# A four-layer graph network on one core: index, attribute and node loads of two passes moved from SyncE's queue to ScalarE's, or asked for by rounds

## The reference, cut to what matters

```python
# layer 2: tensor product with 9 attributes of each edge, summed at the target
summand = _tensor_product(x[i], edge_attr, [w0, w1, w2, w3, w4])
out = jax.ops.segment_sum(summand, j, num_segments=x.shape[0])
return out / float(np.sqrt(NUM_NEIGHBORS))

# layer 3: attention with 64 attributes of each edge
e = (edge_features @ W_edge.T).reshape(num_edges, H, HD)
att = jnp.sum(jnp.concatenate([h[src], h[tgt], e], axis=-1) * a, axis=-1)
...
h_prime = jax.ops.segment_sum(w[:, :, None] * h_src, tgt, num_segments=num_nodes)
```

## Time and profile before

| | |
|---|---|
| three runs, median (lowest to highest) | 7131.51 us (7114.65 to 7133.34) |
| profiled execution | 7100.64 us, span 7098.8 us |
| busy share of the span: PE, DVE, ACT, POOL | 65%, 41%, 35%, 53% |
| mean granted TensorE clock | 0.759 of full speed |
| tensor pass, from its first gather to about its end | 1168 to 3378 us |
| attention pass, the same | 3465 to 6177 us |
| issued DMAs of `e_l` | 196 of 256.0 KB |

### The profile page before, as it was taken

How to read it: one execution, slowest core, us unless ns; L and a number is a source line. 1 busy time by engine, 2 the same in 40 slices (tenths; PEclk the granted TensorE clock), 3 DMA queues, 4 the chain that set the end, 5 groups by cost and what they waited for, 6 DMA issues and landing times. The chain is left out here.

```text
span 7098.8 us, 101641 instructions
## 1 busy us (share of the span) xinstructions
PE 4647.0 (65%) x27975; PEld 3696.9 (52%) x27975; DVE 2932.3 (41%) x9168; ACT 2497.3 (35%) x5991; POOL 3759.5 (53%) x3840
## 2 busy tenths in 40 slices
PE   3389883677777777877465565566555655548886
PEld 2255552465565565656454554455445554525555
DVE  6876553343333333332433333333333333441124
ACT  2434442122222222222455454554555445420003
POOL 0367754555555555555355555555555555446664
PEclk7599996788888888888657666665666666668998
DMA  3133432111111111111222222222222222234442
GB/s 58 58 121 125 144 136 72 45 46 41 40 43 43 40 42 44 43 41 42 54 58 58 63 59 57 58 58 61 59 58 58 58 60 59 47 119 142 149 142 78
DMA packets 412220, 493.79 MB, mean 70 GB/s; under 512 B 253185, under 2 KB 311942, under 8 KB 400897
## 3 DMA queue, kind: packets, MB, share of 16 engines
q0 software_dynamic: 120320, 249.88, 14.1%
q1 hardware_dynamic: 289193, 239.52, 11.4%
q10 hardware_dynamic: 2400, 0.57, 0.1%
HBM read 398.36 MB, written 91.05 MB: 69 GB/s over the span
## 5 line engine op out<-in xcount | busy, mean ns | idle before, releaser
L3597 POOL DMA_INDIRECT rows_l<-table,idx_l x1568 | 1484.0, 946 | 1261.5 <-issue 1022.8
L3101 POOL DMA_INDIRECT rows_l<-table,idx_l x1280 | 1212.5, 947 | 1020.8 <-issue 838.5
L3885 PE MATMUL banks_l<-wrow_l,hot_l 128*128 128x136 f32 x3136 | 778.0, 425 | 1086.7 <-DVE wrow_l L3778 751.8
L3885 PEld LDWEIGHTS banks_l<-wrow_l,hot_l 128*128 128x128 f32 x3136 | 708.5, 321 | 1186.1 <-issue 881.5
L1724 POOL DMA_INDIRECT rows_l<-table,row_idx x896 | 945.3, 1055 | 505.0 <-issue 250.3
L3137 ACT COPY agg_l<-ps_l 128x288 f32<-128x288 f32 x640 | 252.8, 404 | 1553.0 <-PE ps_l L3328 628.7
L3368 PE MATMUL pd_l<-d_row_l,d_hot_l 128*128 128x441 f32 x992 | 527.0, 656 | 304.0 <-ACT d_sums_l L3121 215.7
L3343 PE MATMUL pm_l<-w_mix,agg_l 128*128 128x128 f32 x2880 | 487.9, 301 | 120.1 <-ACT msg_l L3149 73.8
L3328 PEld LDWEIGHTS ps_l<-hoty_l,rows_l 128*128 128x128 f32 x2560 | 444.1, 221 | 164.8 <-issue 163.7
L3635 DVE TENSOR_REDUCE score_l<-bank_s_l 128x32 f32<-128x128 f32 x196 | 57.5, 293 | 1142.0 <-DMA rows_l<-table,idx_l 1133.2
L3328 PE MATMUL ps_l<-hoty_l,rows_l 128*128 128x144 f32 x2560 | 492.8, 320 | 32.4 <-issue 21.9
(11 more groups left out here) (628 smaller groups left out, 8451.9 us busy)
## 6 DMA issues: line engine op xcount, KB each, us to landing
e_l<-in_edge_attr SPq DMA_DIRECT2D x196, 256.0 KB
rows_l<-table,idx_l POOLq DMA_INDIRECT x2848
counts_table<-x_nodes SPq DMA_DIRECT2D x22, 1568.0 KB
x_nodes<-counts_table SPq DMA_DIRECT2D x22, 1568.0 KB
counts_table<-h_nodes SPq DMA_DIRECT2D x21, 1568.0 KB
h_nodes<-counts_table SPq DMA_DIRECT2D x21, 1568.0 KB
rows_l<-table,row_idx POOLq DMA_INDIRECT x896
table<-h_nodes SPq DMA_DIRECT2D x21, 448.0 KB
```

The lines of the kernel that those rows point to most:

```text
L3101: pool.indirect_dma_start(out=rows[:, u, j, :], out_offset=None, in_=table, in_offset=bass.IndirectOffsetOnAxis(ap=idx[:, u, j:j + 1], axi ...
L3597: pool.indirect_dma_start(out=rows[:, u, j, :], out_offset=None, in_=table, in_offset=bass.IndirectOffsetOnAxis(ap=idx[:, u, j:j + 1], axi ...
L3885: last = nc.tensor.matmul(p_sum[:, 0:WROW], hot[:, s, j, :], wrow[:, s, j, :], start=(j == 0), stop=(j == J - 1))
```

## The change

In the tensor pass, `idx` now has room for two rounds instead of four groups. SyncE asks for a round's indices with one DMA (128 x 32 values) instead of four (128 x 8), two rounds ahead, when the four `summed` of the older round are up; GpSimd waits for them once a round. `load_dense` moves from SyncE's queue to ScalarE's, where it stands ahead of `take_parts` in a group's step, and the plan puts at most three nodes at a group instead of six, so 78 groups hold loads where 39 did: groups 0 to 11, and then six groups in a row for each batch (30 to 35, 44 to 49, and so on to 139 to 144). In the attention pass the index and edge attribute loads go to ScalarE: the first four of each at the window's start (`load_first`), and the others at the end of ScalarE's step, behind `widen_hots`, for the group four further on (`load_on`). SyncE keeps `ht` and the gates.

```diff
-                while len(self.loads_at[after]) == 6:
+                while len(self.loads_at[after]) == 3:
...
-        idx = sb("idx", [P, U, J], I32)
+        idx = sb("idx", [P, 2, U * J], I32)
...
-                def load_idx(rnd, u):
-                    at = skip * (U * J) + (rnd * U + u) * J
-                    sp.dma_start(idx[:, u, :], core.near_src[:, ds(sp.snap(at), J)]).then_inc(idx_loaded[u], DMA)
+                def load_idx(rnd):
+                    at = skip * (U * J) + rnd * (U * J)
+                    sp.dma_start(idx[:, rnd % 2, :], core.near_src[:, ds(sp.snap(at), U * J)]).then_inc(idx_loaded[rnd % 2], DMA)
...
-                for u in range(U):
-                    load_idx(0, u)
+                load_idx(0)
                 load_raw(0)
+                load_idx(1)
                 sp.dma_start(rel[:, :, :].rearrange("p g j -> p (g j)"),
                              core.near_rel[:, ds(sp.snap(skip * (U * J)), G * J)]).then_inc(rel_loaded, DMA)
                 sp.dma_start(place0[:, :], core.near_place[:, ds(sp.snap(skip * U), G)]).then_inc(place_loaded, DMA)
-                for rnd in range(R):
+                for rnd in range(R - 1):
                     t = w * R + rnd
-                    for u in range(U):
-                        for i in dense.loads_at[rnd * U + u]:
-                            load_dense(w, i)
-                        if rnd == R - 1:
-                            continue
-                        if u == 0:
-                            sp.wait_ge(raw_turned, START + t + 1)
-                            load_raw(rnd + 1)
-                        for q in range(PAIRS):
-                            sp.wait_ge(rows_loaded[u][q], (t + 1) * (2 * DMA))
-                        load_idx(rnd + 1, u)
-            for u in range(U):
-                sp.wait_ge(idx_loaded[u], START + windows * (R * DMA))
+                    sp.wait_ge(raw_turned, START + t + 1)
+                    load_raw(rnd + 1)
+                    if rnd < R - 2:
+                        for u in range(U):
+                            sp.wait_ge(summed[u], START + t + 1)
+                        load_idx(rnd + 2)
...
-                    for u in range(U):
-                        pool.wait_ge(idx_loaded[u], START + t * DMA + DMA)
-                        pool.wait_ge(summed[u], START + t)
-                        pool.sem_inc(group_begun, 1)
-                        for j in range(J):
-                            pool.indirect_dma_start(
-                                out=rows[:, u, j, :], out_offset=None, in_=table,
-                                in_offset=bass.IndirectOffsetOnAxis(ap=idx[:, u, j:j + 1], axis=0),
-                            ).then_inc(rows_loaded[u][j // 2], DMA)
+                with pool.Fori(0, R // 2) as two:
+                    for s in range(2):
+                        t = w * R + two * 2 + s
+                        for u in range(U):
+                            if u == 0:
+                                pool.wait_ge(idx_loaded[s], START + w * (R // 2 * DMA) + two * DMA + DMA)
...
+                            for j in range(J):
+                                at = u * J + j
+                                pool.indirect_dma_start(
+                                    out=rows[:, u, j, :], out_offset=None, in_=table,
+                                    in_offset=bass.IndirectOffsetOnAxis(ap=idx[:, s, at:at + 1], axis=0),
...
+            def load_dense(w, i):
+                k = dense.caps[i]
+                first = dense.place_of(dense.first[i])
+                cols = slice(first, first + k)
+                if i % B == 0 and dense.batch_of(i) >= 2:
+                    act.wait_ge(dense_hot, START + w * (V // RUN) + dense.columns(dense.batch_of(i) - 2).stop // RUN)
+                    act.sem_inc(batch_begun, 1)
+                at = ds(act.value_load(dense.starts[0:1, i:i + 1], min_val=0, max_val=sh.e - dense.most * P), k * P)
+                loaded = dense_loaded[dense.batch_of(i)]
+                act.dma_start(d_src[:, cols], src[at].rearrange("(p j) -> p j", j=k)).then_inc(loaded, DMA)
+                act.dma_start(d_attr[:, cols, :].rearrange("p j c -> p (j c)"),
+                             attr[at, :].rearrange("(p j) c -> p (j c)", j=k)).then_inc(loaded, DMA)
...
             with act.Fori(0, windows) as w:
+                act.wait_ge(dense_hot, START + w * (V // RUN))
+                act.sem_inc(window_loads, 1)
                 take_y(w * R, 0)
                 for g in groups_of(w):
+                    for i in dense.loads_at[g.index]:
+                        load_dense(w, i)
                     take_parts(g, w)
...
-                    at = ds(sp.snap(sh.first_edge(rnd, u)), GROUP)
-                    sp.wait_ge(e_turned[u], START + t)
-                    sp.dma_start(e64[:, u, :], e_attr[at, :].rearrange("(p j) k -> p (j k)", j=J)).then_inc(e_loaded[u], DMA)
...
-            load_loop(sp, win, sh, src, idx, idx_loaded, rows_loaded, load_others)
+            windows = win.count(sp)
+            with sp.Fori(0, windows) as w_:
+                with sp.Fori(0, sh.rounds) as rnd:
+                    load_others(w_, w_ * sh.rounds + rnd, rnd)
...
+            def load_index(rnd, u):
+                at = ds(act.snap(sh.first_edge(rnd, u)), GROUP)
+                act.dma_start(idx[:, u, :], src[at].rearrange("(p j) -> p j", j=J)).then_inc(idx_loaded[u], DMA)
+
+            def load_edges(rnd, u):
+                at = ds(act.snap(sh.first_edge(rnd, u)), GROUP)
+                act.dma_start(e64[:, u, :], e_attr[at, :].rearrange("(p j) k -> p (j k)", j=J)).then_inc(e_loaded[u], DMA)
+
+            def load_first(w_):
+                for u in range(U):
+                    act.wait_ge(weighed[u], START + w_ * sh.rounds)
+                    load_index(0, u)
+                for u in range(U):
+                    act.wait_ge(e_turned[u], START + w_ * sh.rounds)
+                    load_edges(0, u)
+
+            def load_on(g):
+
+                if g is None or g.near(U) is None:
+                    return
+                load_index(g.near(U).rnd, g.u)
+                load_edges(g.near(U).rnd, g.u)
...
             with act.Fori(0, windows) as w_:
+                load_first(w_)
...
                     widen_hots(g)
+                    load_on(g)
```

More of the change, by code:

```diff
@@ L2970, in tensor_pass @@
         place_loaded = sem("place_loaded")
-        idx_loaded = sems("idx_loaded", U)
+        idx_loaded = sems("idx_loaded", 2)
         raw_loaded = sem("raw_loaded")
@@ L2994, in tensor_pass @@
         batch_begun = sem("batch_begun")
+        window_loads = sem("window_loads")
         started = sem("started")
@@ L3025, in _ @@
             sems_of.open(sp)
[L3027 to L3038, removed]
             windows = count_windows(sp)
@@ L3069, in _ @@
                 sp.dma_start(place0[:, :], core.near_place[:, ds(sp.snap(skip * U), G)]).then_inc(place_loaded, DMA)
-                for rnd in range(R):
+                for rnd in range(R - 1):
                     t = w * R + rnd
-                    for u in range(U):
-                        for i in dense.loads_at[rnd * U + u]:
-                            load_dense(w, i)
-                        if rnd == R - 1:
-                            continue
-                        if u == 0:
-                            sp.wait_ge(raw_turned, START + t + 1)
-                            load_raw(rnd + 1)
-                        for q in range(PAIRS):
-                            sp.wait_ge(rows_loaded[u][q], (t + 1) * (2 * DMA))
-                        load_idx(rnd + 1, u)
-            for u in range(U):
-                sp.wait_ge(idx_loaded[u], START + windows * (R * DMA))
+                    sp.wait_ge(raw_turned, START + t + 1)
[5 more added lines that the diff above has]
+            for s in range(2):
+                sp.wait_ge(idx_loaded[s], START + windows * (R // 2 * DMA))
             for b in range(dense.batches):
@@ L3093, in _ @@
             with pool.Fori(0, windows) as w:
-                with pool.Fori(0, R) as rnd:
-                    t = w * R + rnd
-                    for u in range(U):
-                        pool.wait_ge(idx_loaded[u], START + t * DMA + DMA)
-                        pool.wait_ge(summed[u], START + t)
-                        pool.sem_inc(group_begun, 1)
-                        for j in range(J):
-                            pool.indirect_dma_start(
-                                out=rows[:, u, j, :], out_offset=None, in_=table,
-                                in_offset=bass.IndirectOffsetOnAxis(ap=idx[:, u, j:j + 1], axis=0),
-                            ).then_inc(rows_loaded[u][j // 2], DMA)
+                with pool.Fori(0, R // 2) as two:
+                    for s in range(2):
+                        t = w * R + two * 2 + s
+                        for u in range(U):
+                            if u == 0:
```

(6 more changed lines are left out.)

## The result

The changed kernel took 7159.24 us (median of 7 runs, 7147.87 to 7177.57), the kernel before 7131.51 us (7 runs, 7114.65 to 7149.83): a ratio of 1.0045, 95% interval 1.0027 to 1.0063. It is slower by 28 us, where I had forecast 40 (7170, range 7090 to 7280).

A forecast was written before the change was run, and what follows sets the result against it. Bound: the loop of eight gathers, their landing, then L3635 and L3778, with ScalarE partly late in the tensor pass. Terms −20 + 50 + 15 − 5 = +40 us on the median 7131.51 give 7171, forecast 7170, range 7090 to 7280.

The forecast's parts named there:

- Tensor pass, indices by rounds: Tensor pass start: asking early for two rounds of indices shortens index and raw_l waits; −20 us, bounds 0 and −40.
- Tensor pass, node loads on ScalarE: Tensor pass: three node loads ahead of a group's first copy make ScalarE late; +50 us, bounds 0 and 160.
- 2.7 us stick out: Tensor pass: three node loads take 5.1 us, ScalarE idles 2.4 us before the copy, so 2.7 us remain uncovered.
- half of it counts: Tensor pass: half the groups run at the gather loop's pace with room, so 80 of 160 us count.
- Attention pass, indices on ScalarE: Attention pass: ScalarE asks for indices after L3971, sometimes too late for the gather; +15 us, bounds 0 and 94.
- Attention pass, start: Attention pass start: e_l loads asked for first shorten GpSimd's pause before the fifth group; −5 us, 0 to −8.
- ScalarE hides it all: Rival, tensor and attention passes: ScalarE's idle time covers the loads, only the start's gain remains; 7100 us, chance 0.23.
- As slowly as SyncE: Rival, both passes: ScalarE issues loads as slowly as SyncE between gathers, 3 us a node; +270, 7402 us, chance 0.12.
- The pause shrinks: Rival, both passes: a quiet SyncE shortens the pause after eight gathers by 1 us a group; −356, 6780 us, chance 0.08.

The follow-up runs named there:

- the first pair: The changed kernel against the kernel before, as first measured and profiled, in the slower behaviour: 7159.24 against 7131.51 us, ratio 1.0045.
- the extra reads: Only the tensor pass edited, each node's start read three times instead of once, against the kernel before: 5720.50 us, ratio 1.0469.

## Why the prediction came out as it did

**The total.** 28 us measured against 40 forecast looks closer than the working was. One of the four terms came out, one was right in kind and too large, one was nothing, and one had the wrong sign.

**What bounds the kernel.** The reading held for the behaviour it was made from, and the changed kernel's trace shows the same loop. I wrote that TensorE's release reaches VectorE only once the gathers have landed. That is true of those rows, and it was not a property of the kernel: the same program ran without it and 1668 us shorter. What on the chip differed isn't known.

**Tensor pass, indices by rounds: −20.** Measured −17 in the first thirty groups of one profile each, and the index waits are gone. The mechanism is right; how much of the 17 it made isn't separated from the shorter wait for raw_l and from chance. It hangs on SyncE's slowness at the start, and is 0 where SyncE isn't slow.

**Tensor pass, node loads on ScalarE: +50.** Measured +32 in groups 30 to 159, off by 18. The pitch was 1.54 us where I had 1.7. The mechanism, late copies behind a block of loads, is shown by experiment in the faster behaviour. The traces of the first pair bear it out: in the 66 groups from 30 on that hold loads, TensorE's waits for d_sums_l and msg_l grew from 107 to 158 us, and in the 64 others they stayed (119 and 117). Groups with loads took 74 us more, the others 35 less, so about half was made up. The faster behaviour has the same picture, 62 to 114 and 59 to 58. The weak step is "2.7 us stick out" and "half of it counts": a mean idle time was set against a whole block. What matters is the single copy behind the block, and how far GpSimd is ahead. In the first pair it has no such lead as in the experiments: from the tenth group on, its next gather begins under 1.5 us after the product that frees the buffer in half of the groups, in both kernels. So "free up to 3 us in a block" was not tested there, and the price of a block there is known only as this +32.

**Attention pass, indices on ScalarE: +15.** Wrong. I wrote "ScalarE asks after L3971". It asked 1.9 us before that instruction (now L3997) ended, and no group of the steady pass waited. The term is 0 in the first pair's trace; the attention edit alone gives 0 as well, in a behaviour with 20.5 us to spare. The forecast of 2720 us for this pass (2719.3 measured) came true by luck.

**Attention pass, start: −5.** Wrong in sign. GpSimd's pause before the fifth group went from 12.29 to 13.94, named by the index load, which began at 3560.43, 2.42 us before the gather at 3562.85:

```profile
3560.43 0.34 ACTq L3939 DMA_DIRECT2D idx_l<-in_src  x1
```

```profile
3562.85 0.94 POOL L3600 DMA_INDIRECT rows_l<-table,idx_l  x1 [13.94 <-DMA idx_l<-in_src]
```

The early e_l loads gave nothing: ScalarE's second copy of turned attributes (L4014, before L3988) began only at 3553.98, as the one before at 3510.49, in both kernels once the first 32 gathers were through. Most of the pass's +8.6 is something else: in both kernels GpSimd's own eight gathers take 10.3 instead of 8.8 us in 16 groups, one in twelve, and all 16 lengthened the group now where 11 had. Those 16 groups took 8.9 us more than before, all the others together 0.5 less. Why five were absorbed before is open.

**The rivals.** "ScalarE hides it all" asked for a node below 0.8 us in a block of three, 2.4 us in all. Blocks of 3.1 us cost nothing in the experiments, so this was too strict for that behaviour; 0.8 itself wasn't tried. Its other way out, the same loads apart, I did not see, and there it does hide it all. The rule of the Trainium skill that I cited (DMA: Bandwidth & Descriptors, Issuing engines are not separate DMA queues) says what a second issuing engine saves; here ScalarE's time to issue, 1.54 us a node with its register read, was what cost, as the extra reads show. "As slowly as SyncE" showed in the first groups (1218.31 to 1229.51); over the pass the distance within a block was 1.54 us in the middle. "The pause shrinks" is refuted: with SyncE nearly empty the pause stayed at 4.1.

## What to carry to other kernels

Starting a DMA is work of the engine that starts it, here 1.5 us for a node with its register read. Ask for the instruction right behind it and who waits for that one; then put the starts one at a time into idle stretches that are each longer than one start, since in a block of three they cost 42 us and apart nothing, in the behaviour of the experiments. Look at how far ahead the bounding engine runs before calling a delay free, and take the profile of before more than once: the same program showed two quite different bounds.

## What the runs showed of the hardware

- The same program took 7131 and 5463 us at different times. In the slower behaviour an engine's release reached another engine only after the running gathers had landed (6.5 us against 0.04), and the granted clock was 0.759 against 0.832 in the profiled executions, with TensorE busy for 65% of the span against 78%.
- ScalarE starts a DMA that stands behind a computation before that computation begins: issue at 4570.57, the copy ahead of it in the program at 4571.42. Both DMA records of that step end at 4571.40, before the computation ahead of them does (4572.45), so they delayed nothing; a block of three nodes from 2096.57 to 2101.40 did delay the copy behind it, which began at 2101.53.
- A register read from memory on ScalarE took about 0.5 us, as much as starting a DMA with its address step.
